# Attended values by one 32-bit product, and h turned by DMA in the gate stage, in a fused cross-attention and feed-forward kernel

## The reference, cut to what matters

```python
def reference(x, ctx, Wq, Wkv, w_gate, w_up, w_down):   # x (2,2048,512), ctx (2,128,512), w_* 1536x512
    def attend(h, ctx):
        key, value = split(ctx @ Wkv)
        w = softmax((h @ Wq) @ key.T / sqrt(512))
        return w @ value
    def ffn(h):
        h = act_qdq(h)                       # one scale over the whole tensor: max|h| / 32767
        up = act_qdq(h @ lpbq_dequant(w_up).T)
        gate = act_qdq(h @ lpbq_dequant(w_gate).T)
        sig = fixed_qdq_u16(sigmoid(gate))
        gate = act_qdq(gate * sig)
        return act_qdq(gate * up) @ lpbq_dequant(w_down).T
    x = x + attend(layernorm(x), ctx)
    return x + ffn(layernorm(x))
```

## Time and profile before

| | us |
|---|---|
| median of 3 runs (912.5 to 914.28) | 913.39 |
| the profiled execution | 910.63 |
| its span in the profile | 908.8 |
| TensorE busy in the span | 877.9 (97%) |
| DVE, ACT, POOL busy | 658.6, 567.6, 146.1 |
| first product of the gate stage | 136.92 |

### The profile page before, as it was taken

The page is one execution under the profiler, slowest core; times in us unless marked ns, Lnnn a source line. Parts: engine busy times, 40 slices in busy tenths (PEclk is TensorE's granted clock), DMA queues, the critical chain, the costliest instruction groups (busy, mean ns, idle before and its releaser), DMA issues.

```text
span 908.8 us, 12157 instructions
## 1 busy us (share of the span) xinstructions
PE 877.9 (97%) x4308; PEld 441.8 (49%) x4308; DVE 658.6 (72%) x954; ACT 567.6 (62%) x693; POOL 146.1 (16%) x109
## 2 busy tenths in 40 slices
PE   7999889999999999999999989999799989999998
PEld 5788664444444444444444434444344434444443
DVE  4999896732336243279996859855999998999892
ACT  2379977634454355389997859753689975555330
POOL 0099950077001930000000000000000000000000
PEclk9999999999999999999999998999799999999999
DMA  9822226433459649884339993799987897989872
GB/s 343 327 93 95 93 94 243 162 150 140 163 216 294 227 153 292 322 311 164 137 144 321 370 329 140 258 380 388 404 299 253 283 321 266 397 296 407 314 278 105
DMA packets 92319, 226.57 MB, mean 249 GB/s; under 512 B 31984, under 2 KB 31984, under 8 KB 90096
## 3 DMA queue, kind: packets, MB, share of 16 engines
q1 hardware_dynamic: 91120, 221.80, 67.3%
q10 hardware_dynamic: 1152, 4.19, 1.2%
HBM read 127.40 MB, written 92.27 MB: 242 GB/s over the span
## 4 chain that ended last, share of the span: by engine, by line
PE 55%; issue 14%; DMA 12%; DVE 8%; POOL 6%; ACT 4%; SPq 2%; POOLq 0%; DVEq 0%; ACTq 0%
PE ps L847 27%; PE ps L925 13%; PE ps L880 8%; PE ps L952 3%; DMA big<-product_park 2%; DMA big<-in_L_ffn_w_gate_dram 2%; DMA big<-gate_park 2%; DMA product_park<-big 2%; POOL big L685 2%; DMA big<-sign_park 2%; DVE small L1473 2%; DMA up_park<-big 2%; DVE small L1485 1%; PE ps L942 1%; ACT big L1144 1%
## 5 line engine op out<-in xcount | busy, mean ns | idle before, releaser
L970 ACT ACTIVATE big<-ps 128x1024 f32<-128x1024 f32 (+2 forms) x194 | 153.9, 814 | 194.2 <-PE ps L847 103.2
L880 PE MATMUL ps<-big 128*128 (+1 forms) x1152 | 251.6, 382 | 3.7 <-ACT big L970 3.7
L847 PE MATMUL ps<-big 128*128 (+1 forms) x1152 | 248.8, 379 | 0.5 <-DVE big L1423 0.5
L880 PEld LDWEIGHTS ps<-big 128*128 128x128 f16 x1152 | 113.2, 98 | 141.9 <-issue 7.8
L847 PEld LDWEIGHTS ps<-big 128*128 128x128 f16 x1152 | 112.5, 98 | 136.5 <-DVE big L1423 0.8
L1441 DVE TENSOR_REDUCE small<-big 128x1 f32<-128x1024 f32 (+1 forms) x48 | 58.4, 1219 | 135.1 <-ACT big L970 135.0
L925 PE MATMUL ps<-big 128*128 128x512 f16 x576 | 125.1, 379 | 2.6 <-DVE big L1579 2.6
L925 PEld LDWEIGHTS ps<-big 128*128 128x128 f16 x576 | 56.2, 98 | 71.0 <-issue 3.5
L661 POOL PARTITION_ALL_REDUCE small<-small x9 | 3.6, 405 | 532.9 <-DVE small L1520 182.6
L906 PE MATMUL ps<-big 128*128 128x512 f16 x384 | 86.0, 387 | 2.7 <-ACT big L1177 2.7
L1491 DVE CUSTOM_DVE_ANT_0 big<-big,small 128x1024 f32<-128x1024 int16 x48 | 61.7, 1285 | 7.0 <-DVE small L1485 0.2
(11 more groups left out here) (103 smaller groups left out, 1007.9 us busy)
## 6 DMA issues: line engine op xcount, KB each, us to landing
big<-up_park SPq DMA_DIRECT2D x90, 512.0 KB, 5.7
up_park<-big SPq DMA_DIRECT2D x48, 512.0 KB, 5.2
gate_park<-big SPq DMA_DIRECT2D x42, 512.0 KB, 2.6
big<-gate_park SPq DMA_DIRECT2D x42, 512.0 KB, 6.2
sign_park<-big SPq DMA_DIRECT2D x48, 256.0 KB, 2.2
big<-in_x_dram SPq DMA_DIRECT2D x8, 1024.0 KB, 18.1
x_park<-big SPq DMA_DIRECT2D x8, 1024.0 KB, 3.9
product_park<-big SPq DMA_DIRECT2D x16, 512.0 KB, 5.8
```

Of the source, the lines that this page charges most:

```text
L847: mm = nc.tensor.matmul(ps[:, 2 * (n % 2) + j], w[:, a, k, o:o + P], XT[:, g, b, k], start=(k == 0 and a + b == 0), stop=(k == KC - 1 and ...
L880: mm = nc.tensor.matmul(ps[:, b + j], WU[:, a, k, o:o + P], XT[:, g, c, k], start=(k == 0 and a + c == 0), stop=(k == KC - 1 and c == 1))
L970: return nc.scalar.activation(dst, src, ACT.Copy)
```

## The change

It has three parts. Attended values: V stays in 32-bit as the projection gives it, P is evicted in 32-bit, and one 32-bit product stands for three; the maximum of V, its scaling, the remainders of V and P and one of POOL's reductions go. Turning h: POOL writes normalised h untransposed over all groups (`H`); TensorE turns group 0 only (four tiles, into `first_h`); ACT makes integers of the untransposed groups 1 to 7, and SP turns these with 28 DMA transposes of 128x512 (`turn_half`), two after the sign store of each of the gate product's first 14 units, into `hx`, from which DVE splits. The maximum of |h| is read from what POOL wrote, two tiles at a time, the last two tiles one by one. Places: integers of group g+1 stand in odd units up to the eleventh, splits in odd units from the third on; signs are parked in the early buffer for 18 units; two loops are written out. The numbers of later reductions move down by one.

```diff
-        HT = part(HT0, 16384).rearrange("p (g k t) -> p g k t", g=NG, k=KC)
+        H = part(HT0, 16384).rearrange("p (g i d) -> p g i d", g=NG, i=TI)
...
-        h2 = part(U0 + 4096, 2048).rearrange("p (s d) -> p s d", s=4)
+        first_h = part(U0 + 4096, 2048).rearrange("p (k t) -> p k t", k=KC)
...
+        hx = part(U0 + 2048, 2048).bitcast(I16).rearrange("p (s w) -> p s w", s=2)
...
+        def h_turned(eng, g):
+            eng.wait_ge((wd_turned, wu_turned)[g % 2], 16 * TI * ((g + 1) // 2))
...
+            def turn_half(u):
+                g = u // 2 + 1
+                turned = hx[:, g % 2].rearrange("p (k i t) -> p k i t", k=KC, i=TI)
+                if u % 2 == 0:
+                    sp.wait_ge(hq_d, KC + g)
+                    need(sp, hlo_d, KC + g - 2 if g > 2 else 0)
+                for i in range(u % 2 * 2, u % 2 * 2 + 2):
+                    sp.dma_start(turned[:, :, i], hq[:, g % 2, i * D:(i + 1) * D],
+                                 transpose=True).then_inc((wd_turned, wu_turned)[g % 2], 16)
...
+                    if g * UPG + n < 2 * (NG - 1):
+                        turn_half(g * UPG + n)
...
-                    need(pool, ht_mm, TI * g + i - 3)
-                    nc.gpsimd.tensor_scalar(h2[:, i], X[:, g, i], negm[:, bass.ds(TI * g + i, 1)],
+                    nc.gpsimd.tensor_scalar(H[:, g, i], X[:, g, i], negm[:, bass.ds(TI * g + i, 1)],
...
-            all_max(1, "vmx", "vall")
...
-                pe.wait_ge(plo_d, n // TI + 1)
+                pe.wait_ge(pt_ev, n // TI + 1)
                 need(pe, x2_d_s, n - 1)
-                for a, b in ((0, 0), (0, 1), (1, 0)):
-                    mm = nc.tensor.matmul(ps[:, 5 + n % 2], PTs[:, n // TI % 2, a, n % TI], V[:, b, batch(n // TI)],
-                                          start=(a + b == 0), stop=(a == 1))
+                mm = nc.tensor.matmul(ps[:, 5 + n % 2], PTs[:, n // TI % 2, n % TI], V[:, batch(n // TI)],
+                                      start=True, stop=True)
...
-                if H_LAG <= n < NT + H_LAG:
+                if H_LAG <= n < TI + H_LAG:
                     turn_h(n - H_LAG)
...
             def h_int(g):
-                need(act, hlo_d, g + KC - 2 if g > 1 else 0)
-                nc.scalar.activation(hq[:, g % 2], HT[:, g].rearrange("p k t -> p (k t)"), ACT.Copy,
+                if g == 2:
+                    act.wait_ge(hlo_d, KC)
+                if g > 2:
+                    h_turned(act, g - 2)
+                nc.scalar.activation(hq[:, g % 2], H[:, g].rearrange("p i d -> p (i d)"), ACT.Copy,
                                      scale=col["xinv"]).then_inc(hq_d, 1)
...
-                    if isinstance(g, int) and g == 0 and n + 2 < NG:
-                        h_int(n + 2)
+                    u = g * UPG + n if isinstance(g, int) else NU
+                    if u % 2 and u < 2 * NG - 3:
+                        h_int((u + 3) // 2)
...
             def h_max(n):
-                dve.wait_ge(ht_ev, n + 1)
-                t = (n % TI) * P
-                nc.vector.tensor_reduce(hcol[:, n:n + 1], HT[:, n // TI, :, t:t + P], AX.XY, ALU.max,
+                lone = n + 2 >= NT
+                if not lone and n % 2 == 0:
+                    return
+                dve.wait_ge(h2_d, n + 1)
+                i, j = n % TI, n - NT // 2 + 1 if lone else n // 2
+                nc.vector.tensor_reduce(hcol[:, j:j + 1], H[:, n // TI, i if lone else i - 1:i + 1], AX.XY, ALU.max,
                                         apply_absolute_value=True).then_inc(hcol_d, 1)
...
-                dve.wait_ge(hq_d, g + KC)
-                nc.vector.tensor_copy(hi, hq[:, g % 2]).then_inc(hhi_d, 1)
+                h_turned(dve, g)
+                nc.vector.tensor_copy(hi, hx[:, g % 2]).then_inc(hhi_d, 1)
                 dve.wait_ge(hhi_d, g + KC)
-                nc.vector.tensor_tensor(lo, hq[:, g % 2], hi, ALU.subtract).then_inc(hlo_d, 1)
+                nc.vector.tensor_tensor(lo, hx[:, g % 2], hi, ALU.subtract).then_inc(hlo_d, 1)
-
-            split_h(1)
...
-                    if isinstance(g, int) and g == 0 and n + 2 < NG:
-                        split_h(n + 2)
+                    u = g * UPG + n if isinstance(g, int) else NU
+                    if u % 2 and 3 <= u < 2 * NG:
+                        split_h(u // 2)
```

More of the change, by code:

```diff
@@ L51 @@
 WTOP = 2048.0
+H_ODD = TI * (NG // 2)
+H_EVEN = TI * (NG // 2 - 1)
 KEPT = 23
@@ L286, in build @@
                  "pw0 pw1 pw2 rpw xs xinv fg gt gsc grc ginv fu usc uinv ut urc st ssc sinv src su ot osc "
-                 "oinv orc oo fin vmx vall vg vs vinv okn fin1").split()
+                 "oinv orc oo fin okn fin1").split()
         col = {n: sc[:, k:k + 1] for k, n in enumerate(names)}
@@ L701, in _ @@
                     quant_weights(g + 3, NBLK // 8, 0)
-            all_max(2, "hmx", "hall")
-            all_max(3, "wmx1", "wall1")
+            all_max(1, "hmx", "hall")
+            all_max(2, "wmx1", "wall1")
             pool.wait_ge(w_blk, 2)
             quant_weights(0, NBLK, 8)
-            all_max(4, "wmx2", "wall2")
+            all_max(3, "wmx2", "wall2")
             pool.wait_ge(w_blk, 3)
             quant_weights(0, NBLK, 9)
[L711 to L714, removed]
+            all_max(4, "gmx", "gall")
+            all_max(5, "smx", "sall")
+            all_max(6, "umx", "uall")
+            all_max(7, "omx", "oall")
         @block.tensor
@@ L785, in turn_p @@
             def turn_p(g):
-                need(pe, plo_d, g)
+                need(pe, pt_ev, g)
                 for i in range(TI):
@@ L805, in turn_h @@
                 for k in range(KC):
-                    mm = turn(ps[:, 7, k * P:(k + 1) * P], h2[:, n % 4, k * P:(k + 1) * P])
+                    mm = turn(ps[:, 7, k * P:(k + 1) * P], H[:, 0, n, k * P:(k + 1) * P])
                 mm.then_inc(ht_mm, 1)
@@ L1057, in _ @@
             for k in range(KC):
-                nc.scalar.activation(hq[:, 0, k * 512:(k + 1) * 512], HT[:, 0, k], ACT.Copy,
+                nc.scalar.activation(hq[:, 0, k * 512:(k + 1) * 512], first_h[:, k], ACT.Copy,
                                      scale=col["xinv"]).then_inc(hq_d, 1)
             def h_int(g):
-                need(act, hlo_d, g + KC - 2 if g > 1 else 0)
-                nc.scalar.activation(hq[:, g % 2], HT[:, g].rearrange("p k t -> p (k t)"), ACT.Copy,
+                if g == 2:
[3 more added lines that the diff above has]
+                nc.scalar.activation(hq[:, g % 2], H[:, g].rearrange("p i d -> p (i d)"), ACT.Copy,
                                      scale=col["xinv"]).then_inc(hq_d, 1)
@@ L1088, in take_gate @@
                         act.wait_ge(sign_st[n % 2], 16 * (g * (UPG // 2) + n // 2))
-                    early = isinstance(g, int) and g == 0
-                    if not isinstance(g, int) or g * UPG + n < 2 or g * UPG + n == UPG:
+                    early = u < 3 * UPG
+                    if u < 2 or u == 3 * UPG:
                         act.wait_ge(hq_d, KC + 1 if early else KC + NG - 1)
@@ L1094, in _ @@
             take_gate(0)
-            with nc.scalar.Fori(1, 3) as g:
+            for g in range(1, 3):
                 take_gate(g)
@@ L1371, in _ @@
                     residual(n - X2_LAG)
-                if n % TI == 3 and TI <= n < NT + TI:
-                    p_lo(n // TI - 1)
                 if n + 2 * TI < NT:
@@ L1451, in _ @@
             block_scales(1)
-            common_scale(1, 3)
-            with nc.vector.Fori(1, 3) as g:
+            common_scale(1, 2)
+            for g in range(1, 3):
                 gate_max(g)
@@ L1458, in _ @@
             block_scales(2)
-            common_scale(2, 4)
+            common_scale(2, 3)
             gate_max(4, units=range(2, UPG))
```

65 lines of the change are left out of this document (22 added, 43 removed).

## The result

The changed kernel takes 916.77 us (median of 13 runs, 912.96 to 918.4), the kernel before beside it 912.21 us (13 runs, 909.9 to 914.76): ratio 1.0047, 95% interval 1.0034 to 1.0060. It is slower by about 4.5 us. The forecast was 910.5, with a range of 908.0 to 914.0; sign and range are both wrong.

The account below looks back on a forecast made before the run. TensorE was taken to run the gate product unbroken, its start set by POOL's path; 0.37 + 0.45 + 2.09 = 2.91 us off the median 913.39, other parts at nothing, gave 910.5, range 908.0 to 914.0.

Parts of the forecast that it names:

- Step 3: POOL before the gate product: 0.37 + 0.45 + 2.09 = 2.91 us come off, the product starts at 134.01.
- the narrow slack: Before POOL's eighth group: DVE's variance ready at 120.5, POOL done with group seven at 120.9, slack 0.4 us.
- Steps 1 and 2: Attention stage, 32-bit values and one product per tile: POOL's reduction loses 0.37 us; other reliefs cost at nothing, hidden by POOL.
- Step 4: Gate product, turning h through DMA: SP 0.75 us per transpose (bounds 0.75 to 2.26), splits come late, no stall, cost 0.
- the signs of being wrong: Clock 0.50 at 134 to 140; reduction before 130; TensorE idle between 134 and 210; POOL slower on the same shapes.
- the SP rival: Gate product: narrow transposes cost SP more than 2.26 us each, SP becomes the bound; 915 to 926 us; 11%.
- The rival of the clock: Start of the gate product: TensorE rests 4 to 5 us, its clock falls, costing 2.7 us; 912.2 to 913.2; 22%.
- this rival's last sentence: If transposes don't count as activity, products of tiles 30 and 31 slow by 0.9 us each, over 0.4 slack: some 911.5.
- The rival of DVE setting the reduction: Before the gate product: DVE, not POOL's program change, sets the reduction; it starts near 128, up to 5.5 us gained; 6%.
- The last variance: Before POOL's last group: if late, POOL rests up to 1 us, gain only 1.9 to 2.5, 911.2 us; 8%.

Follow-up runs that it names:

- experiment 3: Kernel before, plus a spare DVE cast and subtraction of 128x2048 after the maxima of units 9, 11 and 13, one loop written out: 919.99 us, ratio 1.0078.
- 2: Changed kernel with POOL's quantising of the up weights in eight pieces of 768 columns instead of one of 6144: 907.6 us, ratio 0.9958.
- 6: Kernel before with POOL's quantising of the up weights in eight pieces of 768 columns and nothing else: 911.46 us, ratio 0.9982.

## Why the prediction was wrong

- **Step 3, POOL's path: right.** Forecast: reduction 6.05 us behind the last tile, at 131.11, product at 134.01; measured 6.25, 130.56 and 133.46. Both rests (0.45 + 2.09) went. POOL's last tiles came at 121.30 instead of 124.94, 3.64 earlier against 2.91 in the sum: the sixth group's already stood 1.13 earlier (112.98 against 114.11), where the sum had 0.37, and 0.64 of that was there at the first reduction (36.70 against 37.34); the narrow slack was just enough: the variance was done at 120.10 (119.44 + 0.66), POOL took it up at 120.19.
- **Steps 1 and 2: right together, not apart.** The reliefs costed at nothing since "POOL hides them" are what let POOL run without rest. The values alone move the start 1.5 us the wrong way, the turning alone by 0.4 to 1.1 the right way, of which up to 0.7 is the scatter of executions. A 32-bit product measures 0.86 us from start to start (112.52 to 113.38), the forecast had 0.90.
- **Step 4, the failing one.** "The splits of group g on DVE come as late"; "I take no stall". I asked whether TensorE would get its groups in time, and whether SP would keep up. I took the splits at their own 1.9 us, without asking what else runs at their new time. They were moved into POOL's quantising, 32 us long (188.79 to 220.81 before), and there four operations of 3.8 us took 8.36 + 6.25 + 3.56 + 11.44 = 29.6 us. Nor did it come through the way I looked at: TensorE had its group; what it lacked was room for results, by the maxima queued behind the split on DVE and the evictions that wait for them. Term costed 0, measured 6.8 (5.3 of rest, about 1.5 of clock behind it). None of the rivals had it; the signs of being wrong did (TensorE idle between 134 and 210, released by an eviction on ACT), and it came at 218.
- The Trainium skill states it (SBUF — State Buffer, the section on SBUF's two separate sides): DVE and GpSimd share a pair of ports as an exclusive lock; who starts first has it for its whole instruction, and the other blocks fully. It names as affected the DVE operations in a two-port mode and, against a GpSimd operation that reads SBUF, those with two inputs from SBUF. The trace agrees: all four long operations end within their own length of the end of POOL's instruction. It also agrees on what is free: the kernel before reads one input per maximum beside the same POOL work, and each of eight took 1.22 us, as ever:

```profile
L1441 DVE TENSOR_REDUCE small<-big 128x1024 f32 x8 | 9.8, 1220 | 27.3 <-ACT big L970 27.3
```

  (groups by line on DVE, 186 to 222 us, kernel before). The subtraction has two inputs. The cast and the small scaling above have one, so of the page's two grounds only the two-port mode is left for them; no run here varies it.
- **Transposes.** Forecast 0.75 us of SP each, measured 1.26 median (bounds 0.75 to 2.26); landing 2.6, under the 5.0 reckoned with. A pair takes 2.5 of a unit's 5.18: the SP rival did not decide.
- **The rival of the clock** came true in the profiled execution beside this, by a shorter rest than I had (2.43, not 4 to 5): the first eviction came at 140.52 against 142.30, 1.78 earlier, so 1.68 of the 3.46 went to the clock. It stood low from about 120 on (0.72 in 119 to 122, 0.50 in 122 to 125) and was at 1.00 again in 128 to 131, under the dummies, as said; then it fell once more behind the rest. The 911.5 of this rival's last sentence isn't the sum of its terms (two products 0.9 later, less 0.4, on 910.5 is 911.9), and its condition did not arise: the clock was 1.00 in 112 to 116, under the products of tiles 30 and 31.
- **The rival of DVE setting the reduction** is excluded (6.25 with DVE done early). The last variance was in time.
- Account by the profiled executions, to the up product: 3.46 gained, 1.7 to the clock at the start, 5.3 stop, 1.5 clock behind the stop: 5.0 later. By the ratios: 7.1 lost where the loss stands alone (experiment 3), 2.2 gained where it is cured (2 against 6), so 4.9 slower; measured 0.47%, 4.3, by the medians 4.6.

Open: whether cast and subtraction each suffice for the stop; how often the clock falls at the start; why each part alone leaves POOL its rests; why the clock is low at the start of the last stage in some executions (32.93 us for its first 144 products) and not in others (31.5 to 32.0).

## What to carry to other kernels

When a change moves an operation in time, read what every other engine does at its new place, not only who waits for it; long POOL instructions are the first to look for when a DVE cast or a two-input operation lands beside them. What a late operation costs is then found by its queue: here the maxima behind it, the evictions that wait for these. If a long POOL instruction can't move, cut it: eight pieces at the same arithmetic turned waits of up to 10 us into waits under 1, and the change from 0.5% slower to 0.4% faster (907.6 us).

## What the hardware showed that I had not expected

- POOL and DVE exclude each other by whole instructions for these operations: up to 10.2 us of waiting for an operation of 1.2 us; and both wait, POOL's 0.83 us piece taking 1.15, its 1.48 one 2.33. POOL's smallest operations did not do it: inside three of 128x4 and 1.01 us (66.71, 77.07, 87.43, kernel before) DVE's two-input operation of the same size kept its 0.16 us (L1303 at 67.45, 77.72, 88.06).
- POOL's change of program costs in both directions. Before the first reduction over partitions and before that of h, both behind ordinary work of POOL, 5.7 to 6.7 us pass in all traces here; the others follow long rests and show nothing. From the reduction's end, at the up weights, back to POOL's first ordinary operation it is 6.7 to 7.7 us ("7.06 <-issue" above). The scales which that operation needs from DVE were done 0.9 us after the reduction (180.48), so some 6.1 us remain with nothing that it waits for.
- A 128x512 transpose by DMA costs SP 1.26 us and lands in 2.6, a 128x1536 one 2.26 and 5.0: three times the size is not three times the cost.
